# Gram-Schmidt on two Gram matrices, attention scores in float32 on four row groups, the second layer moved forward, and no filler matmuls after the first eight

## The reference, cut to what matters

```python
def gram_schmidt(X):
    Q = X
    for i in range(32):
        q = Q[:, i] / (norm(Q[:, i]) + EPS)
        Q = Q.at[:, i].set(q)
        Q = Q.at[:, i + 1:].add(-outer(q, q @ Q[:, i + 1:]))
    return Q
# layer 0: per sequence one of three gelu MLPs, residual, layer norm
# layer 1: adapter 128 -> 32, an expert chosen per sequence, 32 -> 128, residual, layer norm
# layer 2: layer norm, causal attention (16 heads of width 8), layer norm, MLP 128 -> 512 -> 128, gate, residual
# layer 3:
basis = gram_schmidt(U) @ gram_schmidt(V).T
response = (h @ basis) @ basis.T[:, :32] @ resp_w.T + resp_b + safety_bias
return h + strength(mean over the sequence of h) * response
```

## Time and profile before

| | us |
|---|---|
| time, median of 3 runs | 157.54 (156.97 to 163.27) |
| span of the profiled execution | 155.5 |
| median of the runs less the span | 2.0 |
| busy: PE, DVE, POOL, ACT | 131.8, 82.7, 78.5, 56.2 |

### The profile page before, as it was taken

How to read it: one execution, slowest core, us unless ns; L and a number is a source line. 1 busy time by engine, 2 the same in 40 slices (tenths; PEclk the granted TensorE clock), 3 DMA queues, 4 the chain that set the end, 5 groups by cost and what they waited for, 6 DMA issues and landing times.

```text
span 155.5 us, 3723 instructions
## 1 busy us (share of the span) xinstructions
PE 131.8 (85%) x1448; PEld 77.0 (50%) x1448; DVE 82.7 (53%) x306; ACT 56.2 (36%) x130; POOL 78.5 (51%) x168
## 2 busy tenths in 40 slices
PE   6799999998867497499999397999979987898970
PEld 2235754376424132355644175576344933667960
DVE  0510244943688755866765935377564374427413
ACT  8992051123113005820556700232128426311210
POOL 0345257533689947867633725449555974300000
PEclk9999996599999659955558955555899999999555
DMA  4894000000000000000000000000000000000102
GB/s 151 271 361 189 0 4 0 2 0 0 2 0 4 0 0 0 6 0 6 0 4 0 4 4 4 0 0 4 4 0 0 0 4 0 4 0 0 67 0 67
DMA packets 2252, 4.53 MB, mean 29 GB/s; under 512 B 411, under 2 KB 923, under 8 KB 2235
## 3 DMA queue, kind: packets, MB, share of 16 engines
q1 hardware_dynamic: 2235, 4.30, 8.1%
HBM read 3.77 MB, written 0.52 MB: 28 GB/s over the span
## 4 chain that ended last, share of the span: by engine, by line
PE 59%; POOL 16%; DVE 9%; issue 5%; ACT 4%; DMA 2%; SPq 2%; POOLq 0%; DVEq 0%
PE G L286 7%; PE S L311 5%; POOL gsr L891 4%; POOL gsn L885 4%; PE B L331 4%; PE S L276 3%; PE B L371 3%; PE S L453 2%; PE S L444 2%; PE S L446 2%; PE S L445 2%; PE B L347 2%; PE B L345 2%; POOL gsne L888 2%; PE S L435 2%
## 5 line engine op out<-in xcount | busy, mean ns | idle before, releaser
L885 POOL TENSOR_TENSOR gsn<-gsn,half_pos 64x1 f32<-64x1 f32 x32 | 18.7, 584 | 37.3 <-ACT gsq L683 37.3
L683 ACT ACTIVATE gsq<-G 64x128 f32<-64x128 f32 x32 | 8.6, 270 | 55.6 <-PE G L286 55.5
L1041 DVE SCALAR_TENSOR_TENSOR gs_pack<-G,gsf,gs_pack 64x128 f32<-64x128 f32 x32 | 10.9, 341 | 25.5 <-POOL gsf L895 25.3
L286 PE MATMUL G<-gs_pack 32*32 32x128 f32 x128 | 15.6, 327 | 8.5 <-DVE gs_pack L1041 7.3
L1035 DVE CUSTOM_DVE_ANT_0 gsjunk<-gs_pack,G 64x128 f32<-64x128 f32 x32 | 10.8, 336 | 21.1 <-ACT gsq L683 21.1
L891 POOL TENSOR_TENSOR gsr<-gsne,minus_two 64x1 f32<-64x1 f32 x32 | 18.3, 572 | 2.7
L286 PEld LDWEIGHTS G<-gs_pack 32*32 32x32 f32 x128 | 5.0, 115 | 24.6 <-DVE gs_pack L1041 18.3
L444 PE MATMUL S<-kh,qbh 32*128 32x32 f16 x128 | 11.4, 185 | 2.5 <-DVE qbl L1162 2.5
L444 PEld LDWEIGHTS S<-kh,qbh 32*128 32x128 f16 x128 | 10.5, 99 | 2.9 <-DVE qbl L1162 2.8
L445 PEld LDWEIGHTS S<-kl,qbh 32*128 32x128 f16 x128 | 10.7, 101 | 1.7 <-issue 1.7
L276 PE MATMUL S<-filler 128*128 128x512 bf16 x26 | 10.1, 546 | 1.2 <-DVE filler L1078 1.2
(11 more groups left out here) (153 smaller groups left out, 269.7 us busy)
## 6 DMA issues: line engine op xcount, KB each, us to landing
rows<-in_rows SPq DMA_DIRECT2D x1, 576.0 KB, 6.8
xT<-in_xT SPq DMA_DIRECT2D x1, 512.0 KB, 5.3
w<-in_w SPq DMA_DIRECT2D x1, 512.0 KB, 7.6
w<-in_w0b SPq DMA_DIRECT2D x1, 320.0 KB, 3.0
w<-in_w SPq DMA_DIRECT2D x1, 288.0 KB, 5.8
w<-in_w0a SPq DMA_DIRECT2D x1, 256.0 KB, 2.7
xF<-in_xFa SPq DMA_DIRECT2D x1, 256.0 KB, 2.9
xF<-in_xFb SPq DMA_DIRECT2D x1, 256.0 KB, 4.4
```

Source lines behind the costliest of these rows:

```text
L286: j = mm(G[half, 0:P], view(ident, k * R + i, [(0, R)], k * R, R), uv[half, :], start=True, stop=True)
L885: nc.gpsimd.tensor_tensor(gsn[:, i:i + 1], gsn2[:, i:i + 1], half_pos[:], ALU.pow)\
L1041: v.scalar_tensor_tensor(uv[:], G[0:2 * R, 0:P], gsf[:, i:i + 1], uv[:], ALU.mult, ALU.add).then_inc(s["gs_col"], 1)
```

## The change

- Gram-Schmidt keeps its recurrence but runs it on the 32x32 Gram matrices of U and V beside an identity that collects the triangular transform (`gsw`, 64 rows by 64 columns). PE makes the Gram matrices once (`gs_gram`) and multiplies the finished transform with U and V once at the end (`gs_basis`). The 31 steps between are on DVE, with one root on POOL each; PE and ACT take no part in them.
- The scores are one float32 product. The four row groups take turns matmul by matmul. `half_q`, `half_k`, `split_k` and the low halves go; `split_q` masks the float32 query.
- The identity for the transposes comes in a DMA of its own, behind the one of `gs_pack`.
- `L1_up` and `values` write to the bank G, which Gram-Schmidt no longer uses, so that they need not wait for B1 and S3. Layer 1 of half 0 stands between the pieces of `L0_third(1)`; `pick_experts` and `place_experts` stand earlier.
- Of the calls of `keep_warm` only the first is left. The places of the Gram-Schmidt steps in the queues are new, up to six in a row.

```diff
-                for k in range(2):
-                    half = slice(k * R, (k + 1) * R)
-                    j = mm(G[half, 0:P], view(ident, k * R + i, [(0, R)], k * R, R), uv[half, :],
-                           start=True, stop=True)
-                j.then_inc(s["gs_q"], 1)
+            def gs_gram():
+                pe.wait_ge(ld["gs"], 16)
+                for k in range(2):
+                    half = slice(k * R, (k + 1) * R)
+                    j = mm(G[half, 0:R], gs_cols[:, half], gs_cols[:, half], start=True, stop=True)
+                j.then_inc(s["gs_gram"], 1)
...
+                pool.wait_ge(s["gs_row"], i + 1)
+                nc.gpsimd.tensor_tensor(gss[:, i:i + 1], gsb[i % 2][:, 0:1], half_pos[:], ALU.pow)\
+                    .then_inc(s["gs_root"], 1)
...
+            def gs_row(i):
+                v.stream_shuffle(gsb[i % 2][:], gsw[:, i:i + R + 1], [i] * R)\
+                    .then_inc(s["gs_row"], 1)
+            def gs_step(i):
+                one = slice(i, i + 1)
+                row = gsb[i % 2]
+                dve.wait_ge(s["gs_root"], i + 1)
+                v.tensor_tensor(gsu[:, one], gss[:, one], gs_eps[:, one], ALU.add)\
+                    .then_inc(s["gs_den"], 1)
+                dve.wait_ge(s["gs_den"], i + 1)
+                v.reciprocal(gsr[:, one], gsu[:, one]).then_inc(s["gs_rec"], 1)
+                dve.wait_ge(s["gs_rec"], i + 1)
+                v.scalar_tensor_tensor(gsf[:, one], row[:, 0:1], gsr[:, one], gsr[:, one],
+                                       ALU.mult, ALU.mult).then_inc(s["gs_two"], 1)
+                v.scalar_tensor_tensor(gsc[:, one], gsw[:, one], gsr[:, one], gsr[:, one],
+                                       ALU.mult, ALU.mult).then_inc(s["gs_fac"], 1)
+                dve.wait_ge(s["gs_two"], i + 1)
+                dve.wait_ge(s["gs_fac"], i + 1)
+                v.scalar_tensor_tensor(gse[:, one], gsf[:, one], 2.0, gsc[:, one],
+                                       ALU.subtract, ALU.mult).then_inc(s["gs_sym"], 1)
+                v.scalar_tensor_tensor(gsw[:, R:R + 1 + i], row[:, R - i:R + 1], gsc[:, one],
+                                       gsw[:, R:R + 1 + i], ALU.mult, ALU.subtract,
+                                       reverse1=True).then_inc(s["gs_tri"], 1)
+                dve.wait_ge(s["gs_sym"], i + 1)
+                v.scalar_tensor_tensor(gsw[:, i + 1:R], row[:, 1:R - i], gse[:, one],
+                                       gsw[:, i + 1:R], ALU.mult, ALU.add)\
+                    .then_inc(s["gs_res"], 1)
+                dve.wait_ge(s["gs_res"], i + 1)
+                dve.wait_ge(s["gs_tri"], i + 1)
+                if i < R - 2:
+                    gs_row(i + 1)
...
                 for b in range(HB):
-                    qs = qbh[t][rows_, b * P:(b + 1) * P]
-                    qsl = qbl[t][rows_, b * P:(b + 1) * P]
                     sl = slice(b * S, (b + 1) * S)
-                    o = S_[r][:, sl]
-                    mm(o, qs, kh[t][rows_, sl], start=False, stop=False, skip_group_check=True)
-                    mm(o, qs, kl[t][rows_, sl], start=False, stop=False, skip_group_check=True)
-                    i = mm(o, qsl, kh[t][rows_, sl], start=False, stop=(b == HB - 1),
-                           skip_group_check=True)
-                i.then_inc(s["s_ready"], 1)
+                    for r in range(Q):
+                        rows_ = slice(r * A, (r + 1) * A)
+                        i = mm(S_[r][:, sl], qb[t][rows_, b * P:(b + 1) * P], k32[t][rows_, sl],
+                               start=False, stop=(b == HB - 1), skip_group_check=True)
+                        if b == HB - 1:
+                            i.then_inc(s["s_ready"], 1)
...
             to_F("f", 1, ("cF_ready", 2))
-            gs()
             ff_in(1, 0, ("g_ready", 1))
             ff_in(1, 1, ("g_ready", 2))
-            gs()
+            to_F("o", 0, ("fF_ready", 2))
+            ff_in(1, 2, ("g_ready", 3))
+            ff_in(1, 3, ("g_ready", 4))
+            gs_basis()
             ff_out(1, 0, ("u_ready", 1))
```

More of the change, by code:

```diff
@@ L165, in build @@
         res = y
[L167 to L171 removed]
+        gsw = sb("gsw", 2 * R, rows=2 * R)
+        gsb = [sb(f"gsb{k}", R + 1, rows=2 * R) for k in range(2)]
+        gss = sb("gss", R, rows=2 * R)
+        gsu = sb("gsu", R, rows=2 * R)
         gsr = sb("gsr", R, rows=2 * R)
[L173 to L174 removed]
         gsc = sb("gsc", R, rows=2 * R)
         gsf = sb("gsf", R, rows=2 * R)
[L177 removed]
+        gse = sb("gse", R, rows=2 * R)
+        gsjunk = sb("gsjunk", R, rows=2 * R)
+        gsn = sb("gsn", 4, rows=2 * R)
+        gst = sb("gst", R, rows=2 * R)
+        gstT = sb("gstT", R, rows=2 * R)
         uo = sb("uo", P, rows=R)
@@ L190, in build @@
         G = ctx.enter_context(nc.psum_tensor("G", [P, 512], F32))
-        ld = {k: sem("ld_" + k) for k in ("ids", "col", "bf", "w0", "x0", "w0b", "gs", "expert",
+        ld = {k: sem("ld_" + k) for k in ("ids", "col", "bf", "w0", "x0", "w0b", "gs", "ident", "expert",
                                           "x1", "xT", "w1", "rows", "w2", "w3")}
@@ L227, in stepper, with gs @@
             state = [0]
-            def gs():
-                one(state[0])
-                state[0] += 1
+            def gs(n):
+                for _ in range(n):
+                    one(state[0])
+                    state[0] += 1
             return gs
@@ L246, in _ @@
             load(gs_pack[:], "gs", "gs")
+            load(ident[:], "ident", "ident")
             load(exp_pack[:], "expert", "expert")
@@ L333, in L0_second, with L0_third @@
                 i.then_inc(s["pre_z"], 1)
[L335 removed]
+            def L0_third(t, c0, c1, *free):
                 after(free)
@@ L341, in L0_third @@
                 pe.wait_ge(s["h_ready"], 4 * t + 4)
-                for c in range(Q):
+                for c in range(c0, c1):
                     tok = slice(c * P, (c + 1) * P)
@@ L544, in _ @@
             L0_first(0, 3)
-            gs()
             L0_second(0)
-            L0_third(0)
-            gs()
+            pick_experts()
+            L0_third(0, 0, Q)
             L0_third_sr(0)
@@ L576, in _ @@
             L1_up(1, ("y1_sum", 1))
-            gs()
-            keep_warm(S_[2], 5, ("h_ready", 7))
             to_F("h", 0, ("aF_ready", 2))
-            gs()
             queries(0, ("z_ready", 2))
-            keys(0, ("y1_sum", 2))
-            gs()
-            values(0, ("h_ready", 8))
-            gs()
-            scores(0, 0, ("hid_ready", 2))
-            keep_warm(S_[2], 5, ("h_ready", 7))
-            gs()
-            scores(0, 1, ("hid2_ready", 2))
-            scores(0, 2, ("h_ready", 7))
-            gs()
+            keys(0, ("y0_sum", 2))
+            values(0, ("y1_sum", 2))
+            scores(0, ("hid_ready", 2), ("hid2_ready", 2), ("h_ready", 8))
+            to_F("h", 1, ("hF_ready", 1))
+            queries(1, ("q_ready", 1))
+            keys(1, ("k_ready", 1))
             subtract(0, 0)
-            scores(0, 3, ("v_ready", 1))
-            to_F("h", 1, ("hF_ready", 1))
-            gs()
             subtract(0, 1)
@@ L1273, in _ @@
-            gs_dot()
+            gs(2)
+            hidden2(0)
+            sum1(0)
+            stats(1, 0)
+            gs(1)
+            apply(1, 0)
+            affine1(0)
+            stats(2, 0)
             sum0(1)
-            gs_update()
             stats(0, 1)
-            hidden2(0)
-            gs_dot()
-            gs_update()
-            sum1(0)
-            gs_dot()
-            stats(1, 0)
-            gs_update()
-            apply(0, 1)
-            gs_dot()
-            apply(1, 0)
@@ L1337, in _ @@
+            maxima(1, 3)
+            gs(2)
+            sum_x1(0)
+            stats(3, 0)
+            gs(1)
+            apply(3, 0)
             turn(1, 0)
-            gs_dot()
-            maxima(1, 2)
-            sum_x1(0)
-            gs_update()
             turn(1, 1)
-            maxima(1, 3)
-            gs_dot()
-            stats(3, 0)
             turn(1, 2)
             turn(1, 3)
-            gs_update()
-            gs_dot()
-            apply(3, 0)
-            gs_update()
+            gs(2)
```

409 lines of the change are left out of this document (119 added, 290 removed).

## The result

The changed kernel takes 173.17 us in the median of 4 runs (171.20 to 174.21), the kernel before 159.51 beside it (156.97 to 163.27). The ratio is 1.097 with an interval of 1.079 to 1.115: slower, as forecast, and 2.4 us under the forecast of 175.6. The ratio is not the quotient of the two medians, since it leaves out the slower of two groups into which the runs of either kernel fall. The profiled execution has a span of 171.2 us against 155.5.

The account below looks back on a forecast made before the run. It took two chains, Gram-Schmidt and the layers, woven on four in-order queues, as the bound; terms along DVE's queue reached 153.6, plus a 20.0 tail and 2.0 around the span gave 175.6 us, range 158 to 189.

Parts of the forecast that it names:

- A: From the start to the end of half 0's first apply, with experts and a 2.0 us wait: 27.55 us.
- B: Half 0's transposes and `L0_second(1)` at half clock 5.25, pieces of `L0_third` and layer 1 5.7, to apply: 45.05 us.
- D: PE, idle since 41, does transposes and layer 1 at half clock, 9.55 us; queries start at 64.05.
- E: Queries and keys 4.1, values 1.3, masks 1.3, scores 5.7 us, ending at 76.45.
- H: Six steps in a row 11.95, norms and gate 2.15, PE products at half clock 4.85, basis and copies 1.2: 153.6 us.
- The step: One Gram-Schmidt step: six dependent DVE links and a POOL root, 1.45 us of DVE, 2.1 alone against 3.15 before.
- The waits for roots: DVE waits for POOL's root behind `rstd_of`: 2.0 us after `stats`, 4.6 with `skip_sum` on POOL as well.
- The tail: From the first product of the basis to the span's end: 20.0 us, taken as nearly unchanged from before.
- Serial scores: Rival: weight loads do not overlap across row groups, each `scores` 11 to 24 us more, 193 to 218 us; chance 0.10.
- The clock holds: Rival: PE's denser work stays at full clock and steps are at the cheap end, 157 to 165 us; chance 0.20.
- Faster by a short hand-over: Rival: short DVE instructions hand over at the pitch, a step is 0.8 us, 146 us in all; chance 0.08.
- A slow tail: Rival: all of PE's work behind 145 us runs at half clock, 185 us; chance 0.10.

Follow-up runs that it names:

- the run with the three orders: Changed kernel, POOL's roots earlier, half 1's first normalisation and half 0's last output earlier on DVE, `ff_out(1, k)` ahead of the basis: 164.68 us, ratio 1.045.
- with fillers: Changed kernel with 90 filler matmuls put into three long waits of PE: 171.02 us, ratio 1.083.
- the second experiment: Changed kernel with the loops of `scores` swapped, one row group's 16 products after another in place of four in turn: 203.57 us, measured once.
- half 1 forward: Changed kernel with half 1's first sum, statistics and normalisation ahead of half 0's affine and second normalisation on DVE: 171.83 us, ratio 1.084.
- the run with roots first: Changed kernel with the step's root ahead of `rstd_of` and `skip_sum` on POOL at four places: 166.16 us, 1.056 of the kernel before.

## Why the prediction was right, and where it was not

Its stage ends against those of the profile after (E by the start of the first maximum, which waits for the scores):

```
     stage                            predicted   measured
A    first apply ends                     27.55      29.82
B    half 0, layer 1's apply ends         45.05      45.59
C    half 1, first apply ends             54.5       54.92
D    queries start                        64.05      64.56
E    last scores of half 0                76.45      75.31
F    stats of half 0's x1 end            108.35     108.4
G    last apply ends                     133.45     133.48
H    first product of the basis          153.6      153.72
     the tail behind it                   20.0       17.5
```

*The step.* Predicted 1.45 us of DVE and 2.1 a step in a row; measured 1.49 and 2.14. Composing it from a fixed cost, a gap, a pitch and a pointer's price held where POOL ran no wide pass beside it (the last section has the other case). The 1.6 us of eight full costs did not come.

*The waits for roots.* Predicted 2.0 behind `stats` and 4.6 at the end; measured 1.99, 1.97, 2.03 and 3.38. The last was smaller since `skip_sum` needs only the sum: it began at 126.48, beside the statistics, and not behind them. That stage G still ended within 0.03 us of the forecast is luck, other terms in it being too short by as much. That the waits hold the end is shown: taking them away gave 7.0 us.

*A.* 2.3 us too early. DVE waited 0.76 us for `pick_experts` itself, and 1.49 more in `sum0(0)`. I had PE at full clock there. It fell at 16, right behind `pick_experts`. Before, the fall came behind `pick_experts` too, but that stood at 22 us, behind the work that counts. The move of `pick_experts` was in the diff, and I costed it at nothing.

*B* made up for most of it, by luck: 15.8 us from A to B against 17.5 taken. I had the half clock behind PE's wait there, and PE was back at full clock from 28 on (`L0_second(1)` took 1.98 us, not 3.78).

*E.* The scores kept PE busy 6.4 us in half 0, with a gap of 1.1 between, and 6.9 in half 1, against 5.7 taken. Queries and keys ran at full clock, 2.0 against 4.1, and outweighed it. F was then 33.1 us long against 31.9 taken, so that its end agrees to 0.05 us is luck too.

*The tail.* This is the term that was mis-sized: 20.0 taken unchanged from the earlier trace rows, 17.5 measured. Up to the pooling behind `gs_matrix` both kernels take 5.1 us. From there they run the same 56 instructions of PE to the end, the kernel before first:

```profile
140.58:155.50 14.92, 9.86 (x56) 9.19 (x56) 6.05 (x19) 2.47 (x5) 0.00 (x0) 0.62 0.10 35
```

```profile
158.81:171.20 12.39, 7.36 (x56) 6.80 (x56) 5.88 (x19) 2.47 (x5) 0.00 (x0) 0.80 0.12 43
```

All of the 2.5 us lie there and go with the clock. In both it is at 1.00 when the products of `gs_matrix` run; in the kernel before it falls at about 144, 8.5 us behind the first of them, in the changed one at about 166, 12 us behind. That the wide products of `to_F("o", 0)` and `ff_in`, themselves at half clock, brought it back in time is my reading of the window from 147 to 152; why it then lasted longer is not shown, and these are single executions. The changed kernel without steps has the same order there and took 21.2, the run with the three orders 22.0.

*The clock in B, D, F and H.* The sum puts half clock behind PE's longer waits and full clock behind wide work. No run shows such a rule. The first half of it held at 55 and at 147.6 (0.50). But PE was at full clock right behind a wait of 2.66 us at 133.6 (its transposes took 0.63 us, against 1.08 at half clock), it fell at 16 with PE busy throughout, and with fillers it stayed at 1.00 through 5 us of waiting.

*The reading.* The forecast of the time was right and its mechanism was half of the truth. I summed along DVE's queue, and wrote of where the steps stand that this is what costs. Without any steps the changed kernel is still 19.3 us behind the kernel before without its own. So what else was changed carries the loss: the fillers (5.5 us, measured in the kernel before), and, for the rest, the layers' own order and the clock. That rest is not taken apart by runs. The steps together with their waits carry none of it on balance. A sum along one queue counts each stage's end rightly and yet can't say which of two things that overlap would have set it: take the one away and the other is there.

*The rivals.* Serial scores: out, by the rows in the second experiment. The clock holds: out, it is at 0.50 in D and H, and the mean fell. Faster by a short hand-over: out, by the 2.14. A slow tail: out in the changed kernel, real in the run with the three orders.

*Still open.* How the 5.9 us up to the queries divide between `pick_experts` and the place of half 1's work was tried only in part: with half 1 forward, and the steps in, the queries begin at 61.78 in place of 64.56, which is 2.8 us. `pick_experts` in its old place was not run. Nor was the 4.3 + 5.5 us between queries and the second `x1` taken apart: the changed kernel does all four row groups of `scores` before any maximum, so ACT and DVE start late, which is argued from the order and not shown.

## What to carry to other kernels

When a recurrence is woven into other work, measure both kernels with the recurrence left out before you credit or blame it: two runs here turned round the reading that a sum right to 1.4% had given. Put a small result that another in-order engine waits for ahead of the wide passes on its queue (7.0 us here), and see what those passes then run beside. And ask of each idle stretch of TensorE what comes behind it: here a tail of the same work ran at 0.50 in one order and at 0.86 in another, though that the order did it is not shown.

## What the hardware showed that I had not expected

**DVE held by POOL's passes.** In the changed kernel the step behind half 1's first `apply` takes 59.3 - 54.84 = 4.5 us and not 1.49. POOL's passes in that stretch, then DVE's:

```profile
55.06 1.27 POOL L826 TENSOR_TENSOR tmp<-n,rows 128x512 f32<-128x512 f32 x1 [1.80 <-DVE n L971]
...
56.42 1.26 POOL L829 TENSOR_TENSOR a0T<-tmp,b0u 128x512 f32<-128x512 f32 x1
...
57.64 1.26 POOL L835 TENSOR_TENSOR a1bo<-a1T,rows 128x512 f32<-128x512 f32 x1
```

```profile
55.21 1.14 DVE L930 SCALAR_TENSOR_TENSOR gsf<-gsb,gsr 64x1 f32<-64x1 f32 x1
...
56.59 1.10 DVE L936 SCALAR_TENSOR_TENSOR gse<-gsf,gsc 64x1 f32<-64x1 f32 x1
...
57.62 1.30 DVE L938 SCALAR_TENSOR_TENSOR gsw<-gsb,gsc,gsw 64x10 f32<-64x10 f32 x1
```

One column that takes 0.15 to 0.21 us alone takes 1.10 to 1.14, and ends where the POOL pass ends (56.35 and 56.33; 57.69 and 57.68). Each of three passes catches the next such instruction, and the one between them, L932, slips through the gap in 0.20. The same befell `apply` in the run with roots first, 3.14 us against 1.10. The prediction did not ask what DVE would do beside POOL. The Trainium skill states it (SBUF — State Buffer, "SBUF: two separate sides"): DVE and GpSimd have one port pair in common, a DVE instruction with two SBUF inputs needs it against a GpSimd instruction that reads SBUF, and the one that comes second waits for the whole of the other. The trace agrees for the step's instructions, each of which reads two tensors, with 0.9 to 1.1 us per instruction held. `apply` reads one tensor; for it the section names another condition, a two-port mode, and no row here shows whether it was in one.

**The clock behind `pick_experts`.** Its 20 instructions of 32 columns keep PE busy without a gap, and in both kernels the half clock follows: from 16 on in the changed one, where they stand at 12.8 to 15.2 and the window above reads 8.00 us busy at 0.51, and from 24.6 on in the one before, where they stand at 22.0 to 24.3. PE busy is thus no sign that the clock holds. In the two runs without steps the first half-clock instructions likewise come soon behind them, at 14.8 and at about 23. That these instructions are the cause is argued from their moving together, and not shown by a run that has them elsewhere and all else the same.

**Four row groups in turn** at 54 ns an instruction against 184 one after another, each with a weight load of 128 float32 columns. Loads and products were both busy nearly all the time in either run (6.89 and 6.96 of 7.00 us in turn, 23.44 and 23.50 of 23.50 one after another), so which of the two sets the pace is not shown.
